# New weights for a planner that fixes the order of work on all engines of a transformer layer

## The reference, cut to what matters

```python
def attention(x, w_qkv, w_proj, b_proj):            # x: (4, 2048, 256)
    qkv = (x @ w_qkv).reshape(B, S, 3, 16, 16)
    Q, K, V = apply_rope(qkv[:, :, 0]), apply_rope(qkv[:, :, 1]), qkv[:, :, 2]
    attn = jnp.einsum('bqhd,bkhd->bhqk', Q, K) * 16 ** (-0.5)
    attn = softmax(jnp.where(causal, attn, -1e9))
    return jnp.einsum('bhqk,bkhd->bqhd', attn, V).reshape(B, S, 256) @ w_proj + b_proj

def waves(x, theta, phi, theta_noise, phi_noise):
    real = x @ jnp.cos(theta + theta_noise)
    imag = x @ jnp.sin(phi + phi_noise)
    return jnp.sqrt(real * real + imag * imag)

x = x + attention(layernorm(x), ...)
x = x + waves(layernorm(x), ...)
```

## Time and profile before

| | us |
|---|---|
| median of 3 runs | 2019.36 |
| lowest, highest | 2019.03, 2027.15 |
| the profiled execution | 2022.42 |
| its span, first to last instruction | 2020.6 |

### The profile page before, as it was taken

How to read it: one execution, slowest core, us unless ns; L and a number is a source line. 1 busy time by engine, 2 the same in 40 slices (tenths; PEclk the granted TensorE clock), 3 DMA queues, 4 the chain that set the end, 5 groups by cost and what they waited for, 6 DMA issues and landing times.

```text
span 2020.6 us, 38150 instructions
## 1 busy us (share of the span) xinstructions
PE 1971.6 (98%) x12012; PEld 785.2 (39%) x12012; DVE 1566.7 (78%) x4101; ACT 1394.2 (69%) x2687; POOL 861.3 (43%) x1336
## 2 busy tenths in 40 slices
PE   7999999999999999999999999999999999989998
PEld 4333333334433344334343343434443343423334
DVE  4988888988778777797877868788687878677935
ACT  3357767786777676787777677677766777667774
POOL 3632426354443435543364453446434363451232
PEclk8899999999999999999999999999999999999999
DMA  6310212131111221221122111222111222130121
GB/s 134 81 44 13 74 57 73 56 92 57 58 59 55 69 71 59 76 86 62 60 70 70 64 59 54 74 71 90 57 57 60 69 75 75 36 111 7 49 94 63
DMA packets 130762, 133.30 MB, mean 66 GB/s; under 512 B 29434, under 2 KB 105722, under 8 KB 130554
## 3 DMA queue, kind: packets, MB, share of 16 engines
q1 hardware_dynamic: 127728, 128.29, 20.5%
q10 hardware_dynamic: 2832, 2.56, 0.6%
HBM read 38.49 MB, written 25.68 MB: 32 GB/s over the span
## 4 chain that ended last, share of the span: by engine, by line
PE 85%; ACT 4%; POOL 3%; issue 3%; DVE 3%; SPq 1%; DMA 1%; DVEq 0%; POOLq 0%; ACTq 0%
PE banks L1074 23%; PE banks L1059 22%; PE banks L1037 21%; PE banks L981 6%; PE banks L992 5%; PE banks L1019 3%; PE banks L926 2%; ACT probs L1178 2%; DVE chunk_max L1379 1%; SPq L739 1%; PE banks L915 1%; DVE banks L1374 1%; PE banks L908 1%; POOL guess L672 1%; PE banks L1045 1%
## 5 line engine op out<-in xcount | busy, mean ns | idle before, releaser
L1178 ACT ACTIVATE probs<-banks 128x512 f32<-128x512 f32 (+1 forms) x2240 | 1142.3, 598 | 350.8 <-PE banks L1059 311.1
L1379 DVE TENSOR_REDUCE chunk_max<-banks 128x1 f32<-128x512 f32 x1536 | 987.4, 684 | 230.2 <-PE banks L1037 228.1
L1037 PE MATMUL banks<-stack_k,stack_q 96*128 96x512 bf16 (+3 forms) x2560 | 689.2, 350 | 14.4 <-DVE chunk_max L1379 9.3
L1059 PE MATMUL banks<-stack_q,stack_k 99*128 99x512 bf16 (+3 forms) x2560 | 688.5, 350 | 6.1 <-ACT probs L1178 3.0
L1374 DVE CUSTOM_DVE_ANT_0 banks<-banks,row_mask 128x128 f32<-128x128 f32 (+3 forms) x1024 | 484.5, 509 | 113.7 <-PE banks L1037 112.5
L1074 PE MATMUL banks<-probs,v_one 128*17 128x512 f32 (+3 forms) x5120 | 543.3, 533 | 5.6 <-POOL probs L1506 4.9
L1059 PEld LDWEIGHTS banks<-stack_q,stack_k 99*128 99x128 bf16 x2560 | 227.0, 97 | 428.8 <-ACT probs L1178 225.4
L1037 PEld LDWEIGHTS banks<-stack_k,stack_q 96*128 96x128 bf16 x2560 | 233.6, 97 | 354.9 <-DVE chunk_max L1379 94.3
L1506 POOL TENSOR_SCALAR_AFFINE_SELECT probs<-probs 128x512 f32<-128x512 f32 x256 | 163.4, 646 | 251.0 <-ACT probs L1178 250.2
L1074 PEld LDWEIGHTS banks<-probs,v_one 128*17 128x17 f32 x5120 | 110.5, 96 | 273.4 <-ACT probs L1178 134.9
L646 POOL TENSOR_TENSOR turned<-raw,cos_t 128x512 f32<-128x512 f32 x62 | 78.7, 1270 | 236.1 <-ACT raw L1138 228.8
(11 more groups left out here) (158 smaller groups left out, 1153.7 us busy)
## 6 DMA issues: line engine op xcount, KB each, us to landing
stack_q<-parts SPq DMA_DIRECT2D x384, 64.0 KB, 2.6
stack_k<-parts SPq DMA_DIRECT2D x354, 64.0 KB, 2.6
sums<-o_raw SPq DMA_DIRECT2D x64, 256.0 KB, 2.2
rot<-raw SPq DMA_DIRECT2D x236, 64.0 KB, 2.0
xin<-x SPq DMA_DIRECT2D x16, 512.0 KB, 3.8
heads_t<-sums SPq DMA_DIRECT2D x26, 256.0 KB
mid<-x SPq DMA_DIRECT2D x13, 512.0 KB, 3.8
inverse<-inverses SPq DMA_DIRECT2D x26, 256.0 KB
```

The costliest lines, as they stand in the source:

```text
L1037: mm = nc.tensor.matmul(bank[:, n * wide:(n + 1) * wide], stack_q[u % 2][0:SPLIT_ROWS, t, h + n, j * P:(j + 1) * P], stack_k[u % 2][0:SPLI ...
L1059: mm = nc.tensor.matmul(bank[:, a * wide:(a + 1) * wide], stack_k[u % 2][0:ROWS, j // SUB, first + a, (j % SUB) * P:(j % SUB + 1) * P], st ...
L1178: nc.scalar.activation(probs[:, g % PROBS, first:first + many, w0:SPAN], bank, ACT.Exp).then_inc(s_exp, 1)
L1379: nc.vector.tensor_reduce(to, bank[:, 0:count * wide].rearrange("p (h n) -> p h n", h=count), AX.X, ALU.max).then_inc(s_emptied["DVE"], 1)
```

## The change

Seventeen numbers that steer the planner are set anew, and one price in it. `MAX_LEAD`, `QK_LEAD`, `X_LEAD`, `V_LEAD` and `EARLY` say how far ahead of a span's scores its maxima, its projections, the block's loading, the values' projection and the first two units' projections are due; `URGENT` is unit 0's own lead of the maxima. `SLACK`, `MAX_SLACK`, `MAX_FIRST` and `HOLD` bound how early work may start or shift it within a group. `PATIENCE` is the window of choice. `TURN_COST`, `STICK` and `RUN` deal with changes to `values` and back, `TURN_LAG` with the way from the split maximum to its turn, `PACE` and `LAST_PULL` with the last blocks. The price is that of a masked maximum on VectorE. No instruction is added or taken away but fillers; every engine gets the same work in another order and results take other banks.

```diff
-URGENT = 1.0
+URGENT = .526
-MAX_LEAD = 0.56
-QK_LEAD = 0.5
-EARLY = 0.75
-X_LEAD = 0.1
-V_LEAD = 0.5
-SLACK = 0.4
-PATIENCE = 0.1
+MAX_LEAD = .578
+QK_LEAD = .737
+EARLY = .545
+X_LEAD = .189
+V_LEAD = .418
+SLACK = .9
+PATIENCE = .008
-TURN_COST = 0.13
-MAX_FIRST = 0.0
-HOLD = 1.0
-STICK = 0.02
-RUN = 2.0
-TURN_LAG = 1.0
-MAX_SLACK = 0.1
+TURN_COST = .1
+MAX_FIRST = .033
+HOLD = .763
+STICK = 0
+RUN = 4.358
+TURN_LAG = .725
+MAX_SLACK = .02
-PACE = 0.8
+PACE = .924
-LAST_PULL = 0.1
+LAST_PULL = .181
-                with_bank(name, name, "DVE", (0.13 if d == tile // SUB and masks(n) else 0.07 / n) * n + wide / 970, at + step * done / total)
+                with_bank(name, name, "DVE", (0.17 if d == tile // SUB and masks(n) else 0.07 / n) * n + wide / 970, at + step * done / total)
```

## The result

The changed kernel is slower: 2054.84 us (2050.47 to 2057.33) against 2019.19 (2018.7 to 2027.15) for the kernel before on the same chip, a ratio of 1.0167, 95% interval 1.0140 to 1.0194. Its profiled execution took 2053.34 us, with a span of 2051.6 against 2020.6. 2003.5 was forecast, with 2015 as the upper end.

What follows compares the result with a forecast made beforehand. TensorE was taken to bound the steady part. The terms sum to -15.9 us, taking the profiled 2022.42 to 2006.5; set against the median, 3.06 lower, that is 2003.5 us, range 1992 to 2015.

Steps and rivals of the forecast that it cites:

- What bounds the kernel: In the steady part TensorE sets the time, so order can win only what is lost on TensorE's own line.
- Fewer runs: On TensorE, 319 runs of `values` instead of 361, at 0.22 us each: -9.2 us, bounds -8 to -10.5.
- Longer runs: Runs of four or more `values` grow from 15 to 47, each leaving ScalarE without scores: +2 us, bounds 0 to +19.
- rival D: Long runs of `values` starve ScalarE and TensorE then stands still: slower, 2030.5 us, chance 0.05.
- The start: At the kernel's start, first maxima and VectorE's work come earlier: -8 us, bounds -3 to -13.
- Block 11's denominators: Between 1750 and 1800 us, the load of denominators now arrives in time for VectorE: -5 us, bounds -8 to 0.
- Block 0's denominators: Near 430 us, the load stands behind three spans' slots and VectorE waits 3.5 to 5.4 us: +3 us, bounds 0 to +6.
- The end: At the last `values`, a mask wait of 1.9 goes, a bare copy and 19 fillers come: +3.3 us, bounds +1 to +5.5.
- A mask behind GpSimd's other work: At 316.13 us, a mask wait of 1.73 us eases, while new such places come up: -2 us, bounds -5 to +3.
- the rest: Elsewhere, projections and maxima further ahead need no more time on any engine: 0 us, bounds -4 to +6.
- rival C: The small holes close as well and long runs cost nothing: -12 us more, 1991.5 us, chance 0.15.
- The test that I named: Forecast wrong if TensorE's windows between 100 and 1700 us change their work by over 0.3 us in 50.

Runs made afterwards that it cites:

- e1_after_actrot: The changed kernel's order, with the swap's four DMAs issued by ScalarE behind its own copy instead of by SP: 2168.2 us, ratio 1.0714.
- e5_after_slots9: The changed kernel's order, with SP issuing only 9 of each span's 12 slots from unit 2 on (output not the reference's): 2010.32 us, ratio 0.9943.
- e6_after_noswap: The changed kernel's order, without the swap of halves from the sixth span on (output not the reference's): 2008.13 us, ratio 0.9936.

## Why the prediction was wrong, point by point

**What bounds the kernel**: right. TensorE sets the time, and the order can lose only on its line; the 31 us are idle time and clock on it. How the other engines' lists come to stop it is what I had wrong, below.

**Fewer runs, -9.2**: right, -10.5 by the measured 0.25. **Longer runs, +2**: right or less; no run in the trace of the changed kernel shows ScalarE behind them in a way that TensorE feels (4.8 us for L1059 in all, before 3.0), and rival D, my only slow one, was the wrong one.

**The start, -8**: too large for this execution, about -3 by 150 us, which was the lower bound. The first maxima came as said, the first `turn` and the first scores later than 46 and 52, and VectorE was busy for 13.07 of the 25 us from 25 to 50 where I had said over 15:

```profile
29.86 0.61 PE L1037 MATMUL banks<-stack_k,stack_q 96*128 96x128 bf16 x6 [1.21 <-DMA stack_q<-parts]
...
45.78 1.01 PE L1037 MATMUL banks<-stack_k,stack_q 96*128 96x512 bf16 x2 [4.42 <-DMA stack_q<-parts]
...
51.56 0.24 PE L1045 MATMUL banks<-ident_bf,max_parts 128*48 128x128 bf16 x1
...
55.29 0.38 PE L1059 MATMUL banks<-stack_q,stack_k 99*128 99x512 bf16 x1
```

The maxima at 45.78 wait 4.42 us for slots. I had moved the maxima ahead and not asked when their operands land. But this wait is no fixed part of the change. `e1_after_actrot`, `e5_after_slots9` and `e6_after_noswap` run the same instructions up to 50 us, and there the same maxima wait 1.64, 1.41 and 1.39 us, here with 9 slots:

```profile
41.75 0.59 PE L1044 MATMUL banks<-stack_k,stack_q 96*128 96x512 bf16 x2 [1.41 <-DMA stack_k<-parts]
```

In these three the first `turn` comes at 45.0 to 45.5 and the first scores at 48.7 to 49.2, VectorE is busy for 16.7 to 17.2 of the 25 us, and by 150 us `e5_after_slots9` and `e6_after_noswap` are 10.7 and 11.4 us ahead of the kernel before. So the term was sound, and the profiled execution of the changed kernel lost about 6 us of it to slots that landed late: those that SP issued at 33.04 took 9.73 us to land, against 5.8 to 6.4 in the other three. Why, and whether its other executions lost the same, is not known.

**Block 11's denominators, -5**: right, some 6 by the work done. The window that held 45.43 us of TensorE holds 49.18 at full clock. (A sign that I gave with it failed by a little: VectorE waits 2.39 us at L1277 at 1713.)

```profile
1750.00:1800.00 50.00, 49.18 (x319) 23.12 (x317) 39.21 (x102) 34.83 (x70) 30.52 (x43) 1.00 0.18 53
```

**Block 0's denominators, +3**: the right mechanism, at 467 and not at 430, and larger. VectorE waits 6.12 us where I had 3.5 to 5.4, and TensorE 5.04 instead of two thirds of that; with the clock at 0.93 the window loses some 8 us more than before (busy time 49.87 then and 44.79 now, and 3.5 by the clock).

```profile
464.11 0.58 SPq L788 DMA_DIRECT2D squares<-sums  x1
...
466.81 0.55 DVE L1277 RECIPROCAL squares<-squares 128x64 f32<-128x64 f32 x1 [6.12 <-DMA squares<-sums]
...
467.96 0.61 PE L1037 MATMUL banks<-stack_k,stack_q 96*128 96x512 bf16 x1 [5.04 <-DVE chunk_max L1379]
```

The landing was not what went wrong: issue ended at 464.69, and VectorE began 2.1 us later. The Trainium skill, DMA: Bandwidth & Descriptors (the table of the two cost components), has about 2.0 us for the fixed part, in a section on DMAs that GpSimd issues; this load, which SP issued, agrees, and the median of 3.9 of these loads over the whole trace doesn't. Late was SP's queue before it: it issued slots up to 461.5, and two of those groups of six took 5.10 and 5.06 instead of 3.78.

**The end, +3.3**: right. The last `values` begin 48.5 us before the end of the span, against 43.2, less the 1.91 that they no longer wait: +3.4. Not foreseen was a stop ahead of them: VectorE waits 8.95 and 11.41 us for the denominators and inverses of a late block, and TensorE 2.46 us for VectorE at 1969.62.

```profile
2003.10 2.35 PE L1074 MATMUL banks<-probs,v_one 128*17 128x512 f32 x32
2006.16 1.38 PE L1082 MATMUL banks<-ident 128*128 128x128 f32 x10 [0.71 <-ACT o_raw L1185]
...
2011.71 3.96 PE L1082 MATMUL banks<-ident 128*128 128x128 f32 x34
```

**A mask behind GpSimd's other work, -2, bounds -5 to +3**, and **the rest, 0, bounds -4 to +6**: here it failed. The step that failed is "projections and maxima further ahead need no more time on any engine", from which I put the rest at 0. The terms above make, as estimates, -10.5 - 3.1 - 5.9 + 8.3 + 3.4 = -7.8 (the blocks to within about 1 us); the span grew by 31.0; so 38.8 us lie in these two, where I had at most 9. 25.6 of them are TensorE's own longer waits for GpSimd, 2.5 the stop at 1969.62, and the 21 us more at half clock cost about 10 (a rough count, since part of that stands at the start and at block 0). The experiments that free SP or GpSimd give back 44 to 47. In the profiled executions it is 41 and 48, of which some 6 lie before 50 us, where the edits change nothing; the 35 and 42 behind are what the edits bring, part of block 0's wait among them (VectorE waits 1.19 and 3.15 us there).

I had the cause on the page. For block 0 I wrote that three spans' slots would wait for one gate, and that SP needs 7.6 for what the plan takes for 5.4; under rival C even that the planner is blind to it. But I followed this queue only to one load of denominators. In the same queue stand the swaps for GpSimd, and in GpSimd's list behind them 256 masks and 64 split maxima, each of which TensorE needs. The sentence that nothing needs more time is true, and I took it for a reason that they cost nothing. I had looked at VectorE's load by order, and not at GpSimd's and SP's.

The test that I named did show it: from 100 to 1700 us TensorE is busy for 1550.5 us, before 1584.0. That is 1.05 less in each 50, where I had set 0.3.

## What to carry to other kernels

When a statically planned order is changed, take the planner's durations that the trace contradicts (here one line: 5.4 for 7.6) and follow that queue to everyone who waits behind it, not only to the one place where a wait showed before; here longer leads left the order more exposed to such an error (the six leads cost 55 us at the wrong price and 5 at the measured one, though the projections' lead alone cost only 3). Correct that price before tuning the weights. A wait on an engine with much free time is harmless until something short that the bound engine needs stands behind it in its list; look for such neighbours, not for the sum of waits.

## What the runs showed of the hardware that I had not expected

- Four DMA issues on ScalarE took 2.67 us of its time, and moving them there from SP made the kernel 113 us longer, though TensorE's waits for masks nearly vanished.
- Six slots' issues took SP 3.78 us mostly, but 4.88 at 576.32, 5.10 at 434.63 and 5.06 at 452.62, with nothing but issues in the row. Why was not tried.
- The same slots, issued at the same point of the same program, took 9.73 us to land in one profiled execution and 5.8 to 6.4 in three others.
- Thirteen loads of 32 KB had a median of 2.2 us from issue to landing in the kernel before and 3.9 in the changed one, with nothing but the order changed. Why was not tried.
- GpSimd can wait 102 us for one kind of DMA in a kernel that is faster than one in which it waits 24.
